# Two-layer attention and feed-forward kernel: the first output weights gated and split by GpSimd between the pair sums of blocks 12 to 15 and rounded by ScalarE; the second context half of each block rounded directly behind the first

## The reference, cut to what matters

```python
h = _layernorm(x) * (1 + ca) + sa
ctx = softmax(q @ k.T / sqrt(32), causal) @ v        # 16 heads of 32, from h @ W_qkv + b_qkv
x = x + ga * (ctx @ W_out + b_out)                   # the output projection, gated
h = _layernorm(x) * (1 + cb) + sb
x = x + gb * ffn(h)                                  # first layer: silu(h W1) * (h W3), Walsh-Hadamard, W2
# the second layer: linear attention, the same kind of gated output projection, a gated feed-forward part
```

## Time and profile before

| | us |
|---|---|
| median of 3 executions | 2006.1 (2005.12 to 2008.44) |
| the profiled execution's own time | 2000.49 |
| its span, first to last instruction | 1998.7 |
| busy: TensorE, VectorE, ScalarE, GpSimd | 1922.3, 1088.4, 637.8, 541.7 |
| mean granted TensorE clock | 0.993 |

### The profile page before, as it was taken

The page is one execution under the profiler, slowest core; times in us unless marked ns, Lnnn a source line. Parts: engine busy times, 40 slices in busy tenths (PEclk is TensorE's granted clock), DMA queues, the critical chain, the costliest instruction groups (busy, mean ns, idle before and its releaser), DMA issues. The chain is left out here.

```text
span 1998.7 us, 25808 instructions
## 1 busy us (share of the span) xinstructions
PE 1922.3 (96%) x10068; PEld 1386.6 (69%) x10068; DVE 1088.4 (54%) x1834; ACT 637.8 (32%) x1157; POOL 541.7 (27%) x521
## 2 busy tenths in 40 slices
PE   7999999999999998899999999999998989999998
PEld 5677455555555545688888888887886778888886
DVE  5456877666676758754434443445333764434334
ACT  4221455556555563521111111114221251111111
POOL 1121778788776478100000000002001410000000
PEclk9999999999999999999999999999999999999999
DMA  9852422322320112200000010002000011000002
GB/s 324 269 155 100 97 54 55 86 55 54 91 65 16 47 33 85 69 32 32 32 1 32 32 32 1 1 19 74 6 6 12 21 54 32 32 22 22 6 1 84
DMA packets 61882, 111.87 MB, mean 56 GB/s; under 512 B 6032, under 2 KB 21408, under 8 KB 61728
## 3 DMA queue, kind: packets, MB, share of 16 engines
q1 hardware_dynamic: 54304, 85.05, 14.8%
q0 software_dynamic: 7456, 25.18, 4.1%
HBM read 84.77 MB, written 25.44 MB: 55 GB/s over the span
## 5 line engine op out<-in xcount | busy, mean ns | idle before, releaser
L1233 DVE TENSOR_REDUCE part_max<-banks 128x1 f32<-128x512 f32 (+2 forms) x640 | 356.5, 612 | 144.9 <-PE banks L1205 86.5
L1744 ACT ACTIVATE probs<-banks 128x512 f32<-128x512 f32 (+3 forms) x640 | 310.7, 539 | 267.4 <-PE banks L1659 133.9
L1205 PE MATMUL banks<-kst,qst 96*128 96x512 f32 (+2 forms) x640 | 260.7, 415 | 12.4 <-DVE part_max L1233 9.6
L1655 PE MATMUL banks<-qst,kst 98*128 98x512 f32 (+2 forms) x640 | 250.0, 411 | 0.2 <-ACT probs L1744 0.2
L720 DVE TENSOR_TENSOR tokens_a<-banks,tokens_a 128x512 f32<-128x512 f32 x224 | 151.2, 687 | 71.5 <-PE banks L229 70.8
L747 DVE TENSOR_TENSOR tokens_b<-banks,tokens_b 128x512 f32<-128x512 f32 x64 | 44.2, 691 | 252.8 <-ACT tokens_b L662 252.8
L227 PE MATMUL banks<-f_d_hi,f_hid_hi 128*128 128x512 f32 x432 | 170.7, 395 | 7.6 <-DVE tokens_a L720 5.2
L1612 POOL TENSOR_TENSOR early_weights<-probs 128x512 f32<-128x512 f32 (+2 forms) x152 | 160.4, 1084 | 62.2 <-ACT probs L1744 61.8
L1612 POOL TENSOR_TENSOR pairs_own<-probs 128x512 f32<-128x512 f32 (+2 forms) x152 | 158.1, 1070 | 68.2 <-ACT probs L1744 67.9
L227 PE MATMUL banks<-h_hi,f_w_first 128*128 128x512 f32 x448 | 174.6, 390 | 0.0
L229 PE MATMUL banks<-h_hi,f_w_first 128*128 128x512 f32 x448 | 174.3, 389 | 0.0
(11 more groups left out here) (201 smaller groups left out, 3267.0 us busy)
## 6 DMA issues: line engine op xcount, KB each, us to landing
tokens_a<-in_L_wmod SPq DMA_DIRECT2D x12, 1024.0 KB, 7.5
qst<-q_hi SPq DMA_DIRECT2D x32, 256.0 KB, 5.8
kst<-k_hi SPq DMA_DIRECT2D x32, 256.0 KB, 8.2
q_hi<-qk_out_hi POOLq DMA_DIRECT2D x16, 256.0 KB, 3.2
q_lo<-qk_out_lo POOLq DMA_DIRECT2D x16, 256.0 KB, 3.8
k_hi<-qk_out_hi POOLq DMA_DIRECT2D x16, 256.0 KB, 4.7
k_lo<-qk_out_lo POOLq DMA_DIRECT2D x16, 256.0 KB, 4.9
kst<-k_lo SPq DMA_DIRECT2D x16, 256.0 KB, 7.0
```

What stands on the lines that cost most here:

```text
L1205: mm = nc.tensor.matmul(dst[:, 0:wide], qst[n % QS][0:BIASROW, h, P * t:P * t + P], kst[(NB * g + c) % KS][0:BIASROW, h, 0:wide], start=Tr ...
L1233: nc.vector.tensor_reduce(part_max[:, n % 2, ht, c:c + 1], max_bank(slot)[:, 0:wide], AX_X, ALU.max).then_inc(max_read, 1)
L1655: mm = nc.tensor.matmul(dst[:, c0:512], kst[ck % KS][0:BIASROW + 2, h, at:at + P], qst[n % QS][0:BIASROW + 2, h, c0:512], start=True, stop ...
L1744: nc.scalar.activation(probs[:, q % PS, h, c0:512], score_bank(sh)[:, c0:512], ACT.Exp, scale=SCALE).then_inc(exp_done, 1)
```

## The change

GpSimd takes over the gating of the first layer's output weights, their rests, the rests of context halves 0 and 1 and the bias product. They are put into its stream behind the pair sums of single steps (tables `GATED`, `WEIGHT_LO`, `CONTEXT_LO`), the bias product behind the last one. ScalarE takes over the roundings, put behind the exponentials of single steps (`WEIGHT_HI`, `CONTEXT_HI`). VectorE loses `prepare_vector`. The gate is loaded a second time, into `gate_row`, and both it and the raw weights are loaded directly behind the load of n = 15. SyncE waits for the bias product before it loads the first feed-forward weights. In `projection_and_norm`, for both layers, ScalarE rounds half 2b+3 directly behind half 2b+2, ahead of the norm's output. The diff, with unchanged lines left out in places:

```diff
@@ -74,7 +74,7 @@
...
-        OUT0, FFN0, QUERY1, OUT1, FFN1 = 32, 64, 80, 112, 144
+        OUT0, FFN0, QUERY1, OUT1, FFN1 = 48, 80, 96, 128, 160
...
@@ -258,6 +258,7 @@
...
                 multiplied = proj
+                bias_multiplied = bias_gated
 
                 def sync(sp):
                     sp.dma_start(bias_row[:], bias.broadcast_to([P, D])).then_inc(bias_loaded, 16)
@@ -307,21 +308,34 @@
...
-                def prepare_vector(dve, halves):
-                    dve.wait_ge(early_loaded, there)
-                    for k in range(KT):
-                        nc.vector.tensor_tensor(raw[:, k, :], raw[:, k, :], gate, ALU.mult).then_inc(gated, 1)
-                    for k in range(KT):
-                        dve.wait_ge(gated, k + 1)
-                        nc.vector.tensor_copy(w_hi[:, k, :], raw[:, k, :]).then_inc(w_hi_s, 1)
-                    for k in range(KT):
-                        dve.wait_ge(w_hi_s, k + 1)
-                        nc.vector.tensor_tensor(w_lo[:, k, :], raw[:, k, :], w_hi[:, k, :], ALU.subtract).then_inc(w_ready, 1)
-                    for i in range(halves):
-                        src_ready(dve, i // 2)
-                        nc.vector.tensor_copy(c_hi[:, i % 2, :, :], Parts.half(i)).then_inc(hi_s, 1)
-                        Parts.lo_vector(dve, i)
-                    Parts.bias_vector(dve)
+                def gate_gpsimd(pool, k, row):
+                    if k == 0:
+                        pool.wait_ge(early_loaded, there - 16)
+                    nc.gpsimd.tensor_tensor(raw[:, k, :], raw[:, k, :], row, ALU.mult).then_inc(gated, 1)
+
+                def weight_hi_scalar(act, k):
+                    act.wait_ge(gated, k + 1)
+                    nc.scalar.copy(w_hi[:, k, :], raw[:, k, :]).then_inc(w_hi_s, 1)
+
+                def weight_lo_gpsimd(pool, k):
+                    pool.wait_ge(w_hi_s, k + 1)
+                    if k == 0:
+                        pool.wait_ge(gated, KT)
+                    nc.gpsimd.tensor_tensor(w_lo[:, k, :], raw[:, k, :], w_hi[:, k, :], ALU.subtract).then_inc(w_ready, 1)
+
+                def context_hi_scalar(act, i):
+                    src_ready(act, i // 2)
+                    nc.scalar.copy(c_hi[:, i % 2, :, :], Parts.half(i)).then_inc(hi_s, 1)
+
+                def context_lo_gpsimd(pool, i):
+                    pool.wait_ge(hi_s, i + 1)
+                    nc.gpsimd.tensor_tensor(c_lo[:, i % 2, :, :], Parts.half(i), c_hi[:, i % 2, :, :],
+                                            ALU.subtract).then_inc(c_ready, 1)
+
+                def bias_product_gpsimd(pool):
+                    pool.wait_ge(early_loaded, there)
+                    pool.wait_ge(bias_loaded, 16)
+                    nc.gpsimd.tensor_tensor(bias_row[:], bias_row[:], gate, ALU.mult).then_inc(bias_gated, 1)
 
...
@@ -379,12 +393,13 @@
                 if prepared > 1:
                     act.wait_ge(out_p.parts_ready, prepared)
                 for b in range(NB):
-                    if 2 * b + 1 >= prepared:
-                        out_p.hi_scalar(act, 2 * b + 1)
+                    if b == 0 and prepared < 2:
+                        out_p.hi_scalar(act, 1)
                     if b:
                         norm.std_scalar(act, b - 1)
                     if b + 1 < NB:
                         out_p.hi_scalar(act, 2 * b + 2)
+                        out_p.hi_scalar(act, 2 * b + 3)
                     if b:
                         norm.h_scalar(act, b - 1)
                     if b == NB - 2:
@@ -1558,10 +1573,10 @@
                 loads = [(quads_before(n - QS + 1), 1, n) for n in range(QS, NQ)]
                 turns = [(quad_of_turn[n], 0, n) for n in range(1, NQ)]
                 for at, is_load, n in sorted(loads + turns):
-                    if n == NQ - 1 and not is_load:
-                        sp.wait_ge(score_mm, 4 * quads_before(NQ - NB))
+                    (load if is_load else rows_of_max)(n)
+                    if n == NQ - 1 and is_load:
                         sp.dma_start(raw0, tile_rows(a["w_out0"])).then_inc(early_loaded, 16)
-                    (load if is_load else rows_of_max)(n)
+                        sp.dma_start(gate_row, gates[0:1, :].broadcast_to([P, D])).then_inc(early_loaded, 16)
                 sp.wait_ge(score_mm, 4 * quads_before(NQ - 1))
                 out_p.sync(sp)
                 sp.wait_ge(ctx_done, NQ - 1)
@@ -1571,8 +1586,15 @@
                     sp.wait_ge(probs_read, quads_before(NQ - 1) + TB * (b + 1))
                     sp.dma_start(x[:, rows, :], tile_rows(a["L0_attn_x"])[:, rows, :]).then_inc(res_loaded[b], 16)
                 sp.wait_ge(pairs_used, len(pair_index))
+                sp.wait_ge(out_p.bias_multiplied, 1)
                 out_p.next_sync(sp)
                 forward.sync(sp)
+
+            GATED = {(12, 1): (0, 1), (13, 2): (2, 3)}
+            WEIGHT_HI = {(13, 1): (0,), (13, 2): (1,), (14, 0): (2,), (14, 1): (3,)}
+            WEIGHT_LO = {(13, 3): (0, 1), (14, 1): (2,), (14, 3): (3,)}
+            CONTEXT_HI = {(14, 2): (0,), (15, 4): (1,)}
+            CONTEXT_LO = {(14, 4): (0,), (15, 7): (1,)}
 
             def attend_gpsimd(pool):
 
@@ -1626,6 +1648,13 @@
                     if not off_diagonal(s) and n in mixed_at:
                         for step in range(0, 3) if i == 2 * (n % NB) else range(3, 8):
                             butterfly(8 * mixed_at[n] + step)
+                    for k in GATED.get((n, i), ()):
+                        out_p.gate_gpsimd(pool, k, gate_row)
+                    for k in WEIGHT_LO.get((n, i), ()):
+                        out_p.weight_lo_gpsimd(pool, k)
+                    for half in CONTEXT_LO.get((n, i), ()):
+                        out_p.context_lo_gpsimd(pool, half)
+                out_p.bias_product_gpsimd(pool)
                 pool.wait_ge(fw_stored, 16 * (D // FW))
 
             def attend_tensor(pe):
@@ -1743,6 +1772,10 @@
                                 act.wait_ge(pair_ready, 4 * pair_index[s - 2] + h + 1)
                             nc.scalar.activation(probs[:, q % PS, h, c0:512], score_bank(sh)[:, c0:512],
                                                  ACT.Exp, scale=SCALE).then_inc(exp_done, 1)
+                    for k in WEIGHT_HI.get((n, i), ()):
+                        out_p.weight_hi_scalar(act, k)
+                    for half in CONTEXT_HI.get((n, i), ()):
+                        out_p.context_hi_scalar(act, half)
 
             def attend_vector(dve):
 
@@ -1779,7 +1812,6 @@
                             finalize(n - 1, part)
                         for slot in tiles[len(tiles) * part // 4:len(tiles) * (part + 1) // 4]:
                             max_vector(dve, slot)
-                out_p.prepare_vector(dve, 2)
                 for part in range(4):
                     finalize(NQ - 1, part)
 
@@ -1787,12 +1819,13 @@
             second_map = {"o0_c_hi": 0, "f0_hid_hi": 0, "f0_w_first": 8 * KB, "o0_c_lo": 24 * KB, "f0_hid_lo": 24 * KB,
                           "o0_raw": 32 * KB, "n2_z": 32 * KB, "f0_w_second": 32 * KB, "o0_bias": 40 * KB, "n2_h": 42 * KB,
                           "n2_stats": 46 * KB, "n2_mv": 46 * KB + 96, "n2_ve": 46 * KB + 160, "n2_std": 46 * KB + 192,
-                          "n2_rstd": 46 * KB + 224, "o0_w_hi": 48 * KB, "f0_d_hi": 48 * KB, "o0_w_lo": 56 * KB,
+                          "n2_rstd": 46 * KB + 224, "o0_w_hi": 48 * KB, "f0_d_hi": 48 * KB, "o0_w_lo": 56 * KB, "o0_gate": 56 * KB,
                           "f0_d_lo": 56 * KB, "h2_hi": 64 * KB, "h2_lo": 96 * KB}
 
             def alloc(name, shape, dt=F32):
                 return place(name, shape, dt, second_map[name])
             res_loaded = [sem(ctx, f"res_loaded{b}") for b in range(NB)]
+            gate_row = alloc("o0_gate", [P, D])[:]
             raw0 = alloc("o0_raw", [P, KT * D])[:].rearrange("p (k d) -> p k d", k=KT)
             h2_hi, h2_lo = (alloc(n, [P, KT, S], F32R) for n in ("h2_hi", "h2_lo"))
             out_p = project_out(ctx, alloc, "o0_", (a["w1t"], a["w3t"]), a["b_out0"],
```

## The result

The changed kernel took 1996.36 us (median of 4 executions, 1991.59 to 1998.14), the kernel before 2006.62 beside it (2005.12 to 2008.44): ratio 0.9946, 95% interval 0.993 to 0.9962. The forecast was 1995.1 us. On another chip the ratio was 0.9942 (0.9924 to 0.996).

The account below looks back on a forecast made before the run. TensorE bounds nearly everywhere, so only its holes count: 7.65 - 1.95 - 0.8 + 0.2 + 3.6 + 2.3 = 11.0 us, 2006.1 - 11.0 = 1995.1 us. Likeliest case 1992.6 to 1998.6, 8 in 10 range 1991 to 2003.

Parts of the forecast that it names:

- The head: First layer's projection start: first product 4.7 us earlier, plus 2.95 us of clock; 7.65 us gained at tile 3's end.
- Attention: n = 12 to 15: moved work fits idle times of GpSimd and ScalarE; only 0.4 us shows, from half 0's rest.
- The upper bound of 1.5 for the whole: Attention's bounds in the forecast: 0 to 1.5 us more lost to the inserted work.
- signs of being wrong: Exponentials waiting for pair sums, n = 12 to 15 over 1 us longer, or a long VectorE instruction under the bias sums.
- the forecast's window for the landing: Raw weights, issued at about 649.5 behind the load of n = 15, land between 658 and 665.
- `z` of block 0: Ahead of the first transposes: four held instructions add 1.95 us, a 3.1 us hole costs 0.8 of clock; 4.9 remain.
- The order of ScalarE, first layer: Half 7's hole shrinks from 3.61 to 1.2 us; 3.6 us gained, plus 0.2 at half 5.
- Second layer: Half 7 gains 2.8 us; norm output pushed by about 0.6 and 0.95 us; net 2.3 us gained.
- The first: Rival: ScalarE's order brings nothing, only swapping one wait for another; gain 4.9 us, 2001.2 us; chance 0.12.
- The second: Rival: inserted work doesn't fit at n = 12 to 15, costing up to 16.7 us; 2011.8 us; chance 0.05.
- The third: Rival: VectorE's rest of half 2 held until GpSimd's bias sums end at 793.5; 2.25 us slower, 2008.4; chance 0.07.
- The base: Forecast subtracts 11.0 us from the median 2006.1, not the profiled execution 2000.5, which lies 5.6 us under it.

Follow-up runs that it names:

- changed, again: The changed kernel, unedited, profiled a second time; span 1994.6 us, against 1992.8 in its first profile.
- the order alone: Kernel before with only ScalarE's order changed (half 2b+3 rounded directly behind half 2b+2): 1999.19 us, ratio 0.9964.
- the sums waiting: Changed kernel with GpSimd's bias sums of tiles 8 to 15 waiting until block 0's `z` is made: 2000.12 us, ratio 0.9955.
- the preparation done early by VectorE: Kernel before with GpSimd pausing behind its pair sum in (15,2) for two more of ScalarE's exponentials: 2015.75 us, ratio 1.004.
- the preparation alone: Changed kernel with ScalarE's old order in the projections put back, the moved preparation kept: 1999.99 us, ratio 0.9959.

## Why the prediction was right, point by point

From the first pair sum of n = 12 on, in us gained (positive is faster):

| step | forecast | changed | changed, again |
|---|---|---|---|
| head and attention, to the first transposes | 5.7 | 3.7 | 5.4 |
| first layer from there (order, less clock at `z`) | 3.0 | 3.0 | 1.9 |
| second layer's projection | 2.3 | 2.1 | 2.1 |
| all three | 11.0 | 8.8 | 9.4 |
| medians | 11.0 | 10.3 | 12.2 |

The mechanism held step by step, with two sizes off, named below. That the median (1996.4) lies only 1.3 us from the forecast (1995.1) is in part luck: the traced stretches give 8.8 and 9.4 us, and the 1.5 and 2.8 us by which the medians differ more were not traced to anything.

- **The head.** Right. The first product comes directly behind the last sum, at full clock at 770 to 780. From the first product to the transposes 25.02 us; forecast 794.4 - 769.4 = 25.0.
- **Attention.** The term that was most mis-sized. The stretch to the last pair sum was to be 111.64 less 0.95 (last pair sums) plus 0.4 = 111.1 us. It was 111.5 at full clock, which makes the cost 0.8 and not 0.4, and 113.1 in the profile in which the clock fell: 2 us off, 1.6 of them clock. The upper bound of 1.5 for the whole was not wide enough for that, and one of the forecast's signs of being wrong appeared, a span of n = 12 to 15 longer by over 1 us (1.5). Another did not: no exponential waited for pair sums. The 0.4, which was for the rest of half 0, measured 0.2. ScalarE's roundings, taken at 0 as ScalarE is not the bound, showed with 0.3 in both profiles, through the score banks, and 0.25 more stands ahead of all insertions. GpSimd's durations were read rightly (a rest of 1024 columns 2.40 us, estimated at 2.4; a gate or rest of 512 columns 1.3). The raw weights' 5.5 us to landing was not (11.5), but the forecast's window for the landing held.
- **`z` of block 0.** Right: four held instructions, 5.29 us, hole 2.97 (forecast 3.1). The clock fell to half at the hole, for some 3 us in one profile and some 7 in the other, where the forecast took 0.8 us lost of a bound of 1.7. Beside the order alone, whose clock stays at 1.00 there (32.96 us from the transposes to the feed-forward part), the two are 0.5 and 1.6 us longer, so the 0.8 lies between them. With the sums waiting, the hole and the fall at this place went, which shows the cause.
- **The order of ScalarE, first layer.** Right: half 7's hole is 0.86 (forecast 1.2) and the transposes are bound by `z` of block 2. By the order alone the stretch is 3.5 us shorter (36.43 to 32.96; forecast 0.2 + 3.6).
- **Second layer.** Right within 0.2, the pushes among it: the output's waits grew by 0.56 and 0.97, forecast 0.6 and 0.95; putting the rounding behind the output took them away.
- **The rivals.** The first is refuted by the order alone. The second (inserted work doesn't fit) is refuted: at full clock 0.8 us of a possible 16.7 show. The third didn't occur in the changed kernel (the rest of half 2 took 1.29 us in both profiles), but it is real: with the preparation done early by VectorE, a rest of half 2 was held 13.6 us under the bias sums. Its absence here is partly luck, since what decides between held and taking turns is not known, and the reason against it, that such rests got in before, was weaker than the 0.07 suggests.
- **The base.** Subtracting from the median and not from the profiled execution was right: the profile of before was an uncommonly good one, by 2.1 to 4.5 us ahead of n = 12.

## What to carry to other kernels

Work of VectorE that is "idle time anyway" is not free beside a GpSimd that is the bound: either it is held until GpSimd pauses, or it takes turns and slows GpSimd, here by some two thirds of its own length (7.5 us for 11.6); both were seen here from the same instructions. Work of some 12.6 us put into GpSimd's idle times themselves, with some 4.6 us on ScalarE, cost at most 0.8 us at full clock. Before delaying a group of GpSimd instructions to free one VectorE step, look at what VectorE does in the place they move to. And compare a profile with another of the same kernel before putting a few us down to a change: the parts that no kernel here touched differed by up to 4.5.

## What the hardware showed that was not expected

- One VectorE instruction of 0.68 us lasted 29.5 to 29.9 us, through 24 GpSimd instructions, in three of three profiles with the old preparation, and a cast put in its place 29.80; the same cast 3.3 us earlier lasted 1.81.
- TensorE's granted clock fell to the 1.2 GHz level for some 3 us in places where its idle times were under 1 us each, and not in the same places of another execution. Over 29 executions of the kernel before on one chip the span and the mean granted clock go together (correlation -0.85, 2.0 us for 0.001 of clock, the clock between 0.985 and 0.991), so most of the spread between executions of one kernel goes with the clock. A hole does not settle it either: behind half 7's 3.6 us the clock fell in the profile before and stayed at 1.00 in that of the preparation alone.
